# A post-norm attention and ternary feed-forward layer: work moved between VectorE, ScalarE and GpSimd, with a new order of every engine's steps

## The reference

```
sq = elu(q) + 1;  att_mem = sq @ mem / (sq @ z)
sk = elu(k) + 1;  mem += sk^T v;  z += sum(sk)
att = softmax(q k^T / 8) @ v
att = sigmoid(betas) * att_mem + (1 - sigmoid(betas)) * att
y = layernorm(x + att @ Wo)
```

```
h = relu(y @ Wq1^T + b1);  out = layernorm(y + h @ Wq2^T + b2)
```

## Time and profile before

| | us |
|---|---|
| median of 3 runs | 1912.11 |
| the profiled execution's own time | 1912.87 |
| span of the profiled execution | 1910.9 |
| PE busy | 1855.7 (97%) |
| VectorE busy (DVE) | 1449.1 (76%) |
| ScalarE busy (ACT) | 1006.1 (53%) |
| GpSimd busy (POOL) | 794.7 (42%) |
| mean granted TensorE clock | 0.991 |

### The profile page before, as it was taken

How to read it: one execution, slowest core, us unless ns; L and a number is a source line. 1 busy time by engine, 2 the same in 40 slices (tenths; PEclk the granted TensorE clock), 3 DMA queues, 4 the chain that set the end, 5 groups by cost and what they waited for, 6 DMA issues and landing times.

```text
span 1910.9 us, 44707 instructions
## 1 busy us (share of the span) xinstructions
PE 1855.7 (97%) x16575; PEld 1311.8 (69%) x16575; DVE 1449.1 (76%) x2969; ACT 1006.1 (53%) x2426; POOL 794.7 (42%) x790
## 2 busy tenths in 40 slices
PE   5689999999999999999999999999999999999998
PEld 3566677766777766677766677766677766677765
DVE  7867777777777787777777877777777777777774
ACT  5755555555554555554555554545555645555541
POOL 1813344443344444344444344444345444344443
PEclk9889999999999999999999999999999999999999
DMA  8412333223333233233223333323333322333110
GB/s 270 123 23 46 58 61 66 52 49 59 62 59 65 49 53 61 58 60 65 54 45 64 61 59 64 64 38 60 61 59 63 67 38 59 61 58 62 36 23 23
DMA packets 556422, 117.49 MB, mean 61 GB/s; under 512 B 529824, under 2 KB 533808, under 8 KB 555696
## 3 DMA queue, kind: packets, MB, share of 16 engines
q1 hardware_dynamic: 556208, 114.64, 29.4%
HBM read 50.54 MB, written 16.80 MB: 35 GB/s over the span
## 4 chain that ended last, share of the span: by engine, by line
PE 80%; SPq 7%; DVE 6%; DMA 3%; issue 2%; ACT 1%; POOL 1%; DVEq 0%; POOLq 0%; ACTq 0%
PE bank L431 12%; PE bank L430 12%; PE bank L444 8%; PE bank L445 8%; SPq L1551 7%; PE bank L280 6%; PE bank L282 6%; PE bank L281 6%; PE bank L413 3%; PE bank L411 3%; PE bank L412 3%; PE bank L368 3%; DMA amax_row<-amax_dram 2%; PE bank L294 2%; PE bank L347 2%
## 5 line engine op out<-in xcount | busy, mean ns | idle before, releaser
L430 PE MATMUL bank<-yt,w1t 128*128 128x256 f16 x2048 | 453.9, 273 | 0.0
L431 PE MATMUL bank<-yt,w1t 128*128 128x256 f16 x2048 | 453.9, 273 | 0.0
L1141 ACT ACTIVATE prob<-bank,exp_bias,gscalars 128x128 f32<-128x128 f32 x512 | 227.6, 455 | 356.6 <-DVE exp_bias L723 347.7
L444 PE MATMUL bank<-w2t,arena 128*128 128x512 f16 x1024 | 388.4, 379 | 0.0
L445 PE MATMUL bank<-w2t,arena 128*128 128x512 f16 x1024 | 388.1, 379 | 0.0
L1187 ACT ACTIVATE arena<-bank,b_scaled,wscalars 128x256 f32<-128x256 f32 x512 | 262.9, 569 | 213.4 <-PE bank L431 156.3
L858 DVE CAST arena<-arena 128x512 f16<-128x512 f32 x256 | 154.8, 605 | 89.9 <-ACT arena L1187 89.1
L1317 POOL TENSOR_TENSOR att_mem<-att_mem,gate_in 128x512 f32<-128x512 f32 x60 | 83.1, 1385 | 330.1 <-DVE att_mem L762 318.7
L430 PEld LDWEIGHTS bank<-yt,w1t 128*128 128x128 f16 x2048 | 200.5, 98 | 23.3 <-issue 0.3
L431 PEld LDWEIGHTS bank<-yt,w1t 128*128 128x128 f16 x2048 | 200.3, 98 | 22.7
L1395 POOL TENSOR_TENSOR arena<-arena 128x512 f16<-128x512 f32 x128 | 155.3, 1213 | 87.6 <-DVE arena L858 87.6
(11 more groups left out here) (191 smaller groups left out, 4392.9 us busy)
## 6 DMA issues: line engine op xcount, KB each, us to landing
rows<-in_L_attn_x SPq DMA_DIRECT2D x32, 512.0 KB, 3.6
out_rows<-rows SPq DMA_DIRECT2D x64, 256.0 KB, 2.3
x_blocks<-in_L_attn_x SPq DMA_DIRECT2D x248, 64.0 KB, 2.8
sk<-sk_t SPq DMA_DIRECT2D x480, 32.0 KB, 2.0
att_dot<-att_mem SPq DMA_DIRECT2D x480, 32.0 KB, 2.0
y_blocks<-rows SPq DMA_DIRECT2D x480, 32.0 KB
arena<-in_L_ffn_W SPq DMA_DIRECT2D x6, 1024.0 KB, 5.5
w2t<-in_L_ffn_W SPq DMA_DIRECT2D x2, 1024.0 KB, 13.3
```

The lines of the kernel that those rows point to most:

```text
L430: pe.matmul(ps[:, c], w1t[:, k, cols], yt[:, g % 2, :, k], start=k == 0, stop=False)
L431: ins = pe.matmul(ps[:, c], w1t[:, k, cols], yt[:, g % 2, :, KT + k], start=False, stop=k == KT - 1)
L444: pe.matmul(banks[own][:], h_hi[:, f, toks], w2t[:, f, :], start=f == 0, stop=False)
L1141: ins = act.activation(prob[:, t, at], ps[:, c], ACT.Exp, scale=gcol(g, G_EXP), bias=exp_bias[:, t, at:at + 1], accum_out=row_sum[:, t, h: ...
```

## The change

Seven things are changed together.

1. `normalise` goes from VectorE to ScalarE, as an activation Identity with a scale and a bias; GpSimd makes the bias (`shift`) in a further small step of `inverse_std`.
2. `h_relu` writes the high part for odd j itself, by a second pair of activations from PSUM; VectorE's `h_split` is called for even j only, and `h_rest` waits for ScalarE instead of VectorE.
3. For g > 0, `xt_hi` also scales x in place, and the low part of x is a subtraction on GpSimd.
4. The exponent's bias is one operation for a tile (`exp_bias_of`) instead of one for each half.
5. All compares are on VectorE, with two mask buffers of each kind in place of four, which lie in half of `yt`; W2's blocks use banks 6 and 7.
6. PE turns blocks 0 to 7 in turn 0, 8 to 27 in turn 1 and 28 to 31 in turn 2. VectorE compares 0 to 15 in turn 0 and 16 to 31 in turn 1. The first `ffn_up` waits for W1's blocks alone.
7. Every engine's list has a new order. PE's, without the weights:

The new code of the helpers (the lists are left out; context is cut):

```
@@ -132,8 +133,8 @@
-        wbelow = yt[:, 0].rearrange("p t k n -> p (t k n)").rearrange("p (b n) -> p b n", b=4)
-        wabove = yt[:, 1].rearrange("p t k n -> p (t k n)").rearrange("p (b n) -> p b n", b=4)
+        masks = yt[:, 1].rearrange("p t k n -> p (t k n)").rearrange("p (m b n) -> p m b n", m=2, b=2)
+        wbelow, wabove = masks[:, 0], masks[:, 1]
@@ -217,6 +218,10 @@
+        def turned_bank(n):
+            return banks[n % 2 if n < NBLOCKS // 2 else 6 + n % 2][:].rearrange("p (j c) -> p j c", j=4)
@@ -253,17 +258,19 @@
             def turn_w(n):
-                ps = banks[n % 2][:].rearrange("p (j c) -> p j c", j=4)
+                ps = turned_bank(n)
-                pe.wait_ge(sem["above"], n + 1)
-                pe.wait_ge(sem["below_pool" if n % 2 else "below"], n // 2 + 1)
+                if n == NBLOCKS // 2:
+                    pe.wait_ge(sem["hscale"], 1)
+                    pe.wait_ge(sem["thr_chain"], 2)
+                pe.wait_ge(sem["masks"], n + 1)
-                    pe.matmul(ps[:, j], wabove[:, n % 4, cols], ident16[:], start=True, stop=False)
-                    ins = pe.matmul(ps[:, j], wbelow[:, n % 4, cols], minus16[:], start=False, stop=True)
+                    pe.matmul(ps[:, j], wabove[:, n % 2, cols], ident16[:], start=True, stop=False)
+                    ins = pe.matmul(ps[:, j], wbelow[:, n % 2, cols], minus16[:], start=False, stop=True)
             def ffn_down(g, t, piece):
+                if g == 0 and piece == 0:
+                    pe.wait_ge(sem["wput"], NBLOCKS)
@@ -664,13 +673,13 @@
             def turn_x(g, t):
+                dve.wait_ge(sem["amax"], g + 1)
             def xt_lo(g, t):
-                if not 0 <= g < NG:
-                    return
-                dve.scalar_tensor_tensor(out=xt[:, t, KT:2 * KT], in0=in_cols(x_blocks, t) if g else x_bank(t), scalar=gcol(g, G_SCALE), in1=xt[:, t, 0:KT],
+                dve.scalar_tensor_tensor(out=xt[:, t, KT:2 * KT], in0=x_bank(t), scalar=gcol(g, G_SCALE), in1=xt[:, t, 0:KT],
@@ -716,12 +725,15 @@
+            def exp_bias_of(g, t):
+                if not 0 <= g < NG:
+                    return
-                    dve.wait_ge(sem["pexp"], by_half(g - 1, t, half))
-                dve.wait_ge(sem["rowmax"], by_half(g, t, half))
-                dve.tensor_scalar(exp_bias[:, t, hs], row_max[:, t, hs], gcol(g, G_EXP), -1.0, ALU.mult,
-                                  ALU.mult).then_inc(sem["exp_bias"], 1)
+                    dve.wait_ge(sem["pexp"], by_half(g - 1, t, 1))
+                dve.wait_ge(sem["rowmax"], by_half(g, t, 1))
+                dve.tensor_scalar(exp_bias[:, t], row_max[:, t], gcol(g, G_EXP), -1.0, ALU.mult, ALU.mult).then_inc(sem["exp_bias"], 1)
@@ -832,14 +844,6 @@
-            def normalise(g, t, which):
-                if not 0 <= g < NG:
-                    return
-                r = rows[:, g % NX, t]
-                dve.wait_ge(sem[f"rstd{which}"], by_t(g, t))
-                dve.tensor_scalar(r, r, mean_var[:, which, t, 0:1], rstd[:, which, t:t + 1], ALU.subtract,
-                                  ALU.mult).then_inc(sem[f"norm{which}"], 1)
@@ -854,11 +858,12 @@
             def h_split(g, j):
+                if n == 0:
+                    dve.wait_ge(sem["masks"], NBLOCKS)
-                if j % 2 == 0:
-                    dve.wait_ge(sem["h_hi"], n + 1)
-                    dve.tensor_tensor(lo, h32[:, n % NH32], hi, ALU.subtract).then_inc(sem["h_dve"], 1)
+                dve.wait_ge(sem["h_hi"], n // 2 + 1)
+                dve.tensor_tensor(lo, h32[:, n % NH32], hi, ALU.subtract).then_inc(sem["h_dve"], 1)
@@ -906,11 +911,10 @@
             def compare(n):
-                if n >= 4:
-                    dve.wait_ge(sem["wturn"], n - 3)
-                if n % 2 == 0:
-                    dve.tensor_scalar(wbelow[:, n % 4], src, w(BELOW[m]), None, ALU.is_lt).then_inc(sem["below"], 1)
-                dve.tensor_scalar(wabove[:, n % 4], src, w(ABOVE[m]), None, ALU.is_gt).then_inc(sem["above"], 1)
+                if n >= 2:
+                    dve.wait_ge(sem["wturn"], n - 1)
+                dve.tensor_scalar(wbelow[:, n % 2], src, w(BELOW[m]), None, ALU.is_lt)
+                dve.tensor_scalar(wabove[:, n % 2], src, w(ABOVE[m]), None, ALU.is_gt).then_inc(sem["masks"], 1)
@@ -1092,7 +1086,10 @@
             def xt_hi(g, t):
-                act.activation(xt[:, t, 0:KT], in_cols(x_blocks, t) if g else x_bank(t), ACT.Copy, scale=gcol(g, G_SCALE)).then_inc(sem["xt_hi"], 1)
+                ins = act.activation(xt[:, t, 0:KT], in_cols(x_blocks, t) if g else x_bank(t), ACT.Copy, scale=gcol(g, G_SCALE))
+                if g:
+                    ins = act.activation(x_blocks[:, t], x_blocks[:, t], ACT.Copy, scale=gcol(g, G_SCALE))
+                ins.then_inc(sem["xt_hi"], 1)
             def exponentials(g, t, half):
-                act.wait_ge(sem["exp_bias"], by_half(g, t, half))
+                act.wait_ge(sem["exp_bias"], by_t(g, t))
@@ -1164,10 +1161,17 @@
             def yt_hi(g, t):
-                else:
+                elif g == 1:
+            def normalise(g, t, which):
+                if not 0 <= g < NG:
+                    return
+                r = rows[:, g % NX, t]
+                act.wait_ge(sem[f"shift{which}"], by_t(g, t))
+                act.activation(r, r, ACT.Identity, scale=rstd[:, which, t:t + 1], bias=shift[:, which, t:t + 1]).then_inc(sem[f"norm{which}"], 1)
@@ -1176,16 +1180,23 @@
             def h_relu(g, j):
+                    act.wait_ge(sem["masks"], NBLOCKS // 2 + 4)
+                if n == 1:
+                    act.wait_ge(sem["masks"], NBLOCKS)
+                if g and j == 1:
+                    act.wait_ge(sem["ffn2"], by_t(g - 1, 1))
+                    if j % 2:
+                        ins = act.activation(h_hi[:, f], ps[:, c], ACT.Relu, scale=w(H_SCALE_Y), bias=b1_scaled[:, f:f + 1])
@@ -1345,6 +1363,9 @@
             def inverse_std(g, t, which):
+                pool.wait_ge(sem[f"rstd{which}"], by_t(g, t))
+                pool.tensor_scalar(shift[:, which, t:t + 1], mean_var[:, which, t, 0:1], rstd[:, which, t:t + 1], -1.0,
+                                   ALU.mult, ALU.mult).then_inc(sem[f"shift{which}"], 1)
@@ -1359,6 +1380,12 @@
+            def xt_lo(g, t):
+                if not 0 < g < NG:
+                    return
+                pool.wait_ge(sem["xt_hi"], by_t(g, t))
+                pool.tensor_tensor(xt[:, t, KT:2 * KT], in_cols(x_blocks, t), xt[:, t, 0:KT], ALU.subtract).then_inc(sem["xt"], 1)
@@ -1391,18 +1418,8 @@
             def h_rest(g, j):
-                pool.wait_ge(sem["h_hi"], n + 1)
+                pool.wait_ge(sem["relu"], n + 1)
-            def compare(n):
-                m, i, b = block_place(n)
-                src = ffn_raw(m, i)[:, b * 512:(b + 1) * 512]
-                if n in (1, 17):
-                    pool.wait_ge(sem["threshold"], m)
-                pool.wait_ge(*ffn_raw_loaded(m, i))
-                if n >= 4:
-                    pool.wait_ge(sem["wturn"], n - 3)
-                pool.tensor_scalar(wbelow[:, n % 4], src, w(BELOW[m]), None, ALU.is_lt).then_inc(sem["below_pool"], 1)
```

More of the change, by code:

```diff
@@ L1281, in _ @@
                         put_w(n)
+                yt_hi(g - 1, 0)
+                yt_hi(g - 1, 1)
+                if g == 1:
+                    for n in range(24, 28):
+                        put_w(n)
+                p_split(g, 1, 0)
+                normalise(g - 2, 0, 1)
                 p_split(g, 1, 1)
@@ L1285, in _ @@
                         put_w(n)
-                yt_hi(g - 1, 1)
+                h_relu(g - 1, 0)
+                if g == 1:
+                    for n in range(28, 32):
+                        put_w(n)
                 xt_hi(g + 1, 0)
+                h_relu(g - 1, 1)
+                h_relu(g - 1, 2)
+                xt_hi(g + 1, 1)
                 if g == 0:
@@ L1298, in _ @@
                 h_relu(g - 1, 3)
+                normalise(g - 2, 1, 1)
         @block.gpsimd
```

390 lines of the change are left out of this document (175 added, 215 removed).

## The result

The changed kernel takes 1925.1 us (median of 4 runs, 1923.99 to 1925.23) against 1911.7 for the kernel before in the same comparison (1909.08 to 1915.68): a ratio of 1.0070, 95% interval 1.0056 to 1.0084. It is 13 us slower. The forecast was 1907 with a range of 1895 to 1924: the direction was wrong, and the time lies above the range.

The account below looks back on a forecast made before the run. PE was taken as the bound, busy 1855.7 of 1910.9 us, leaving only idle and lower-clock time to win. Turn's end -4, start -2.0 and drain +0.4 took 1912.87 to 1907 us, range 1895 to 1924.

Parts of the forecast that it names:

- (a): Turn's end: ffn_up(g-1,0) ahead of attend(g,1) covers waits with 1.77 us; gain 0 to 7.5 us, taken as 4.
- (b): elu(k) before the earlier update_memory: 1.7 us of cover normally, a 1.1 us wait in slow turns; nothing added.
- (c): Next group's x at the first projection: ScalarE and GpSimd finish it in time by 0.5 us; no gain possible.
- Rival 2: x's low part from GpSimd late at the first projection, every turn from 2; middle 1925 us, chance 0.24.
- VectorE's relief: Norm, half the casts and x's low part leave VectorE: 230 us off 1449, near 1220 us busy.
- this collision at x alone: GpSimd's subtraction of x's low part may collide with VectorE on shared SBUF interfaces; 0.5 us more each favours the slower case.
- (d): y's chain: slower norm and a 0.28 us GpSimd step, but as many PE steps as before; nothing.
- The start: Turns 0 and 1: late weight blocks fill PE's waits; +1 - 8 + 10.8 - 5.8 = -2.0 us, ends -14 and +9.
- under 3 was the sign: Sign of a right forecast: the window from 96 to 144 us has under 3 us of PE idle time.
- +1 - 8: Turn 0: first scores later, taken as +1 us; 8 fewer blocks bring PE to turn 1's projections 8 us earlier.
- Rival 3: The start doesn't fill: block groups stop PE and VectorE waits for masks; 1914 us, chance 0.12.
- The tail: Drain after PE's last work gets GpSimd's step and the slower norm: 0.28 + 0.16 = +0.4 us.

Follow-up runs that it names:

- e1: Changed kernel with read_scale(g,1) moved behind p_split(g,1,0) in VectorE's list: 1918.96 us, ratio 1.0037 to the kernel before.
- b1: Kernel before the change with only the norms moved to ScalarE, GpSimd making the shift: 1907.56 us, ratio 0.9975.
- b2: Kernel before the change with only relu's high part for odd j written by ScalarE: 1922.58 us, ratio 1.0052.
- f2: Changed kernel without its last 12 weight blocks, with four mask buffers of each kind instead of two: 1919.97 us, ratio 1.0028.
- e3: Changed kernel with turn 0's Wo maximum, Wo split and ffn_scale put back behind q's splits: 1923.42 us, ratio 1.0052.
- f1: Changed kernel with GpSimd again making the mask below for odd blocks of 0 to 15: 1934.3 us, ratio 1.0104.
- g3: Changed kernel with turn 0's exponentials of t = 1 ahead of the last sum of absolute values and block copies: 1926.06 us, ratio 1.0062.
- h1: Changed kernel with turn 0's compares of blocks 12 to 15 moved ahead of x's last steps on VectorE: 1926.48 us, ratio 1.0065.
- e2: Changed kernel with the high-part casts of odd j back on VectorE in the last two groups: 1924.24 us, ratio 1.0057.

## Why the prediction was wrong, by its own steps

**(a) The turn's end: -4 predicted, +4.3 measured for the middle. This step failed.** Its error, 8.3 us, is the largest of the sum. It asked only what `ffn_up(g-1,0)` in front of `attend(g,1)` covers (1.77 us), and took the splits as ready when they had been ready before. It didn't walk VectorE's new list: `read_scale(g,1)`, which waits for PE, now stands ahead of `p_split(g,1,0)`. In numbers, VectorE waits until 1048.51, has 2.7 us of small steps and then 1.3 us of splits, and PE comes 0.27 us too early, in nearly every turn. e1 removes the wait by moving that step and gets 6 us back. What the step said of the disturbed turns came true in number, their excess fell from 8.0 to 2 us, but not shown by its cause. It had `ffn_up` cover the 0.4 us waits of L368, and L368 is `read_memory`, which has no `ffn_up` in front of it in the new list either (the 3.6 us are those of `attend`, for which the profile names no engine). In b1 and b2 most of these waits went in the old order, with the norms or half of the casts off VectorE and nothing else changed. In the changed kernel `move_y` follows the maximum's write by 0.4 us for 0.9, as in b1.

**(b) elu(k) for the memory and (c) x: nothing predicted, and nothing lost.** `update_memory` has 0.9 us of waits in the whole middle, and no projection of k waits for x there. Rival 2, the slower case of the prediction, named the right sign and almost the right time (1925) for a wait that doesn't occur; that is luck.

VectorE's relief is half of what was forecast: 1330 us busy, where near 1220 were expected. Steps that stayed on VectorE grew where the new order put them beside GpSimd's. Two of them, before and after (columns as in the earlier trace rows):

```profile
L693 DVE SCALAR_TENSOR_TENSOR sq_t<-exp_tmp,relu_tmp 128x512 f32<-128x512 f32 x64 | 47.1, 735 | 0.0
L861 DVE TENSOR_TENSOR arena<-arena 128x512 f16<-128x512 f32 x128 | 90.4, 706 | 4.4
```

```profile
L702 DVE SCALAR_TENSOR_TENSOR sq_t<-exp_tmp,relu_tmp 128x512 f32<-128x512 f32 x64 | 74.3, 1161 | 0.0
L866 DVE TENSOR_TENSOR arena<-arena 128x512 f16<-128x512 f32 x128 | 115.2, 900 | 4.4
```

In all but a few turns `at_lo` runs beside one of each. With L758 (287 to 701 ns) and L656, a maximum of 128 x 1 numbers beside `gate_mix` and x's low part (149 to 904 ns), it is about 100 us in all. GpSimd's own steps got shorter (`at_lo` 1162 ns for 1495). The Trainium skill (GPSIMD Engine Reference, section Specifications) says that GpSimd shares its SBUF interfaces with VectorE, in contention with VectorE instructions in a two-port mode or with two SBUF inputs. The trace agrees for the two rows above and L656, which read two tensors in SBUF; L758 and a compare of the start (1.45 us beside GpSimd's low parts of x, 0.48 otherwise) read one, and no run here shows their mode. The prediction asked for this collision at x alone. Only at L758 is it seen beside a wait of PE, and its price alone was not measured.

**(d) y: nothing, drain +0.4.** The drain grew by 0.63: the norm on ScalarE takes 813 ns, not the 719 taken from another activation with a scale alone.

**The start: -2.0 predicted (ends -14 and +9), +4.45 measured. This step failed too, inside its ends.** The fill was right in kind: the late blocks are 5.2 us cheaper at the milestone, 3 by the times, and 96 to 144 us have the clock at 1.00, but 8.9 us idle where under 3 was the sign. The count of blocks is off: 24 blocks stood ahead of turn 1's first projection and 16 do now, so 16 and not 12 follow up to k of group 2, where 8 did. The other terms were too small. The prediction had +1 - 8 for turn 0 and for PE's earlier arrival in turn 1. Measured: the first projection of turn 1 starts at 87.70 for 87.44, with 8 blocks fewer behind it. So the time of the 8 blocks that left this stretch turned into waits. The windows of 62 to 88 us show it: PE is busy 15.67 us there, and was 19.77, so 4.1 us more are idle. Rival 3 ("the start doesn't fill") had the right outcome for the start, +5, but not the cause: two masks instead of four cost nothing in the first 20 blocks (f2). What does cost is not one wait. Four single moves (e3, f1, g3, h1) changed k of group 2 by -0.3, +8.2, +1.8 and +2.4 us in a profile, and the time of all but f1 by nothing that the intervals can tell. Blocks, probabilities and x go through VectorE, PE and ScalarE in turn, and each list has them in the same new order, so that mending one hands the wait to the next. That last sentence is shown for blocks 12 to 15 (h1) and only argued for the rest. So the cause of the start's loss stays open, and so does the order of the three lists that would give the 9.7 us back.

**The tail: +0.4 predicted, +3.4 measured (2.74 + 0.63).** The term for ScalarE's four activations behind an odd j was missing. The prediction used their duration (2.0 us for four) only in (c) and didn't set it against PE's 1.77 us for an `ffn_up` where several stand in a row. b2 shows the same cost in the old order, 0.36 us in 29 places; e2 gives 1.65 us back.

Two of the rivals' sums have slips. Rival 2 prices (b)'s 1.1 us in ten turns at 4, and they are 11. Rival 3 leaves the middle as it is and yet takes off the 4 of (a); without them it is 1918.

The sum with the measured terms: 4.28 + 4.45 + 2.74 + 0.63 = 12.1 us, and 1910.9 + 12.1 = 1923.0, the span.

## What to carry to other kernels

When an engine's list is reordered, walk the new list of each engine once with the trace's start times, and look for a step that waits for the bottleneck engine and now stands ahead of a step that the bottleneck waits for. Taking work off an engine with room needn't gain anything; of the four parts tried alone here one gained (the norms, behind which `move_y` is issued), and three lost 0.5 to 2.6% in the old order: a part may only be priced together with its place in the list. A mend in the list of one engine may not help where the neighbouring engines have the same order (h1). And a step that stays can get longer by what runs beside it, which a sum of moved work leaves out.

## What the runs showed that was not expected

- Gaps of 0.27 us on PE didn't show as waits or as idle time. The turn's spacing in SyncE's queue showed 0.35 us a turn that the wait list didn't have.
- A VectorE operation of 128 x 8 numbers took 1.15 us beside a GpSimd operation of 128 x 512 and ended with it; 0.28 us is what it takes otherwise.
- An activation of 128 x 512 with both a scale and a bias from memory takes 813 ns in place; with a scale alone it takes 716 ns in place (L1091 of the changed kernel), 719 into float16.
- The clock got better in a kernel that got slower. From 96 to 144 us it is 1.00 with 8.9 us idle, where it was 0.89 with 5.8 us idle.
